# Wide cross-attention layers: SyncE's order of stores and fetches, three buffers for packed and turned probabilities, and VectorE's reciprocal ahead of its block transpose

## The reference

```python
def _L1_xattn_ref(hidden_states, encoder_hidden_states, Wq, Wk, Wv, Wo, bo):
    q = hidden_states @ Wq
    k = encoder_hidden_states @ Wk
    v = encoder_hidden_states @ Wv
    ...
    scores = jnp.einsum('bhsd,bhkd->bhsk', q, k) * Dh ** -0.5
    probs = jax.nn.softmax(scores, axis=-1)
    out = jnp.einsum('bhsk,bhkd->bhsd', probs, v)
    out = out.transpose(0, 2, 1, 3).reshape(B, S, H * Dh)
    return out @ Wo + bo
```

## Time and profile before

| | us |
|---|---|
| median of 3 runs | 1755.21 (1746.41 to 1760.99) |
| the profiled execution | 1738.73 |
| its span | 1736.9 |
| TensorE busy | 1450.2 (83%) |
| VectorE busy | 961.7 (55%) |
| ScalarE busy | 594.1 (34%) |
| GpSimd busy | 55.2 (3%) |

### The profile page before, as it was taken

How to read it: one execution, slowest core, us unless ns; L and a number is a source line. 1 busy time by engine, 2 the same in 40 slices (tenths; PEclk the granted TensorE clock), 3 DMA queues, 4 the chain that set the end, 5 groups by cost and what they waited for, 6 DMA issues and landing times.

```text
span 1736.9 us, 22426 instructions
## 1 busy us (share of the span) xinstructions
PE 1450.2 (83%) x9148; PEld 939.3 (54%) x9148; DVE 961.7 (55%) x1742; ACT 594.1 (34%) x850; POOL 55.2 (3%) x68
## 2 busy tenths in 40 slices
PE   5988798888988888798887888898887858877987
PEld 3555485355555455666473555455545528875444
DVE  5555603677767775233526667777762467733424
ACT  4512011455545544011014445545541105531302
POOL 0000000000000000000000000000000012220000
PEclk9998899989999998979788899999998859988987
DMA  5110153366667665600122566666764204552000
GB/s 198 76 49 1 49 200 140 109 182 169 174 166 187 173 174 160 197 1 1 73 97 64 154 184 179 170 172 173 190 182 149 106 25 154 199 203 75 1 1 12
DMA packets 102854, 215.86 MB, mean 124 GB/s; under 512 B 7776, under 2 KB 73312, under 8 KB 95200
## 3 DMA queue, kind: packets, MB, share of 16 engines
q1 hardware_dynamic: 101600, 206.04, 39.7%
q0 software_dynamic: 1152, 8.39, 1.3%
HBM read 146.77 MB, written 67.63 MB: 123 GB/s over the span
## 4 chain that ended last, share of the span: by engine, by line
PE 57%; DVE 19%; DMA 12%; issue 5%; SPq 4%; ACT 2%; POOL 1%; POOLq 0%; ACTq 0%; DVEq 0%
PE ps L237 26%; DMA ring<-blocks 11%; SPq L453 3%; DVE wk L941 3%; PE ps L1668 3%; DVE wk L944 3%; PE ps L1669 3%; PE ps L1670 3%; DVE wk L929 3%; PE ps L1553 2%; PE ps L1648 2%; PE ps L1696 2%; PE ps L1681 2%; PE ps L1612 2%; PE ps L1649 2%
## 5 line engine op out<-in xcount | busy, mean ns | idle before, releaser
L929 DVE TENSOR_REDUCE wk<-ps 128x1 f32<-128x1024 f32 x128 | 156.2, 1220 | 204.5 <-PE ps L1654 203.2
L599 ACT ACTIVATE wk<-wk 128x1024 f16<-128x1024 f32 x128 | 184.1, 1439 | 217.8 <-DVE wk L936 188.6
L590 ACT ACTIVATE wk<-ps,wk 128x1024 f32<-128x1024 f32 x128 | 142.1, 1110 | 169.2 <-DVE wk L929 168.2
L941 DVE SCALAR_TENSOR_TENSOR wk<-wk 128x1024 f16<-128x1024 f32 x128 | 181.3, 1416 | 10.4 <-ACT wk L599 10.1
L1668 PE MATMUL ps<-ring,ctx_keys 128*128 128x256 f16 x240 | 84.8, 353 | 107.7 <-DMA ring<-blocks 107.7
L944 DVE STREAM_TRANSPOSE wk<-wk 128x1024 f32<-128x1024 f32 x128 | 159.4, 1246 | 4.4
L237 PE MATMUL ps<-wk,ring 128*128 128x128 f32 (+3 forms) x896 | 133.7, 313 | 29.5 <-issue 11.6
L237 PEld LDWEIGHTS ps<-wk,ring 128*128 128x128 f32 x896 | 119.0, 211 | 43.3 <-issue 25.1
L237 PE MATMUL ps<-ring,wk 128*128 128x256 f32 (+2 forms) x456 | 112.4, 401 | 4.8 <-DVE wk L1130 1.7
L237 PE MATMUL ps<-wk 16*64 16x64 f32 (+8 forms) x1172 | 93.5, 249 | 15.6 <-ACT wk L708 8.1
L1553 PE MATMUL ps<-cst 128*128 128x512 f16 x362 | 100.9, 435 | 1.2 <-PE ps L237 0.3
(11 more groups left out here) (328 smaller groups left out, 2320.4 us busy)
## 6 DMA issues: line engine op xcount, KB each, us to landing
blocks<-wk SPq DMA_DIRECT2D x128, 512.0 KB, 3.1
ring<-units SPq DMA_DIRECT2D x34, 1024.0 KB, 6.0
xn_both<-blocks SPq DMA_DIRECT2D x128, 256.0 KB, 5.5
ring<-blocks SPq DMA_DIRECT2D x120, 256.0 KB, 5.3
ring<-experts SPq DMA_DIRECT2D x16, 1024.0 KB, 7.0
ring<-context SPq DMA_DIRECT2D x16, 384.0 KB, 3.8
wk<-context SPq DMA_DIRECT2D x16, 384.0 KB, 3.2
wk<-blocks SPq DMA_DIRECT2D x8, 256.0 KB, 5.8
```

What stands on the lines that cost most here:

```text
L590: ACTE.activation(blocks, bank(2 * (t % 2), 2, 4, 128), ACT.Exp, bias=WNM[:, t % 4:t % 4 + 1], accum_out=WRS[:, t % 4:t % 4 + 1]).then_inc ...
L599: ACTE.activation(WPH[:, t % 2, :], WXP[:, t % 2, :], ACT.Identity, scale=WRI[:, t % 4:t % 4 + 1]).then_inc(xa_PH, 1)
L929: DVE.tensor_reduce(WNM[:, t % 4:t % 4 + 1], bank(2 * (t % 2), 1024), X, ALU.max, negate=True).then_inc(xa_max, 1)
L941: DVE.scalar_tensor_tensor(WPL[:, t % 2, :], WXP[:, t % 2, :], WRI[:, t % 4:t % 4 + 1], WPH[:, t % 2, :], ALU.mult, ALU.subtract).then_inc ...
```

## The change

Six edits, the first four inside the wide layers:

1. The packed probabilities have three places, t % 3, at 6144, 7168 and 10252 of `wk`, which grows by 452 columns; `weights_high(t)` waits for the store of unit t-3.
2. The turned groups have three places in turn: the slot of Wo, `xn_both`, the slot of Wq; groups 30 and 31 take `xn_both` and Wq's slot. The fetch of group g waits for `attend_low(g-3)` (g-2 for the last two). Wo is loaded after unit 59's store and the fetch behind it, once `attend_low(27)` is done.
3. The fetch of group g stands behind the store of unit 2g + 1, one store earlier in SyncE's list.
4. VectorE does `recip(s)` before the block transpose of unit s-1, which has become a function of its own.
5. The constants are 316 columns narrower: `nhalf` has 4 columns where it had 64, and the two biases share one place of 256 columns. SyncE loads the second bias ahead of unit `L2x_k`, after the first has been added.
6. GpSimd waits for that load before it adds the bias.

```diff
+        def packed_weights(t):
+            return wv((6144, 7168, 10252)[t % 3], 1024)
+
+        def weight_halves(t):
+            v = packed_weights(t).bitcast(F16).rearrange("p (b h) -> p b h", h=2)
+            return v[:, :, 0], v[:, :, 1]
...
             if g == 0:
                 return wv(8192, 2, 1024)
-            if g % 2:
+            place = g % 3 if g < 30 else g - 29
+            if place == 1:
                 return xn_both[:, :].rearrange("p (j m) -> p j m", j=2)
-            return unit("L1x_q" if k == 0 else "L2x_q", 0, 2, 1024)
+            u = "L1x_" if k == 0 else "L2x_"
+            return unit(u + ("q" if place == 2 else "o"), 0, 2, 1024)
...
-                if g >= 2:
-                    sp.wait_ge(xa_Z, 2 * (32 * k + g - 2) + 2)
+                if g >= 4:
+                    sp.wait_ge(xa_Z, 2 * (32 * k + g - (3 if g < 30 else 2)) + 2)
...
-            def turn_weights(k):
-
+            def turn_weights(k, n):
+
+                sp.wait_ge(units_used, n - NSLOT + 1)
                 for t in range(64):
                     store_blocks(k, t)
-                    if t >= 2 and t % 2 == 0:
-                        fetch_turned(k, t // 2 - 1)
-                fetch_turned(k, 31)
+                    if t % 2 == 1:
+                        fetch_turned(k, t // 2)
+                    if t == 59:
+                        sp.wait_ge(xa_Z, 2 * (32 * k + 27) + 2)
+                        load(n)
...
-                load(n)
+                if UNITS[n] == "L2x_k":
+                    sp.wait_ge(xa_bo, NT)
+                    sp.dma_start(C("Lx_bo"), const_d[:, NCONST:]).then_inc(consts_loaded, 16)
                 if UNITS[n] in ("L1x_o", "L2x_o"):
-                    turn_weights(0 if UNITS[n] == "L1x_o" else 1)
+                    turn_weights(0 if UNITS[n] == "L1x_o" else 1, n)
+                else:
+                    load(n)
...
                     act.wait_ge(xa_recip, 64 * k + t + 1)
-                    if t >= 2:
-
-                        act.wait_ge(xa_stored[j], 16 * (32 * k + g))
-                    ACTE.activation(WPH[:, t % 2, :], WXP[:, t % 2, :], ACT.Identity,
+                    if t >= 3:
+
+                        act.wait_ge(xa_stored[(t - 3) % 2], 16 * (32 * k + (t - 3) // 2 + 1))
+                    ACTE.activation(weight_halves(t)[0], WXP[:, t % 2, :], ACT.Identity,
...
+
+                def block_transpose(t):
                     dve.wait_ge(xa_PL, 64 * k + t + 1)
-                    DVE.transpose(WPB[:, t % 2, :], WPB[:, t % 2, :]).then_inc(xa_block, 1)
+                    DVE.transpose(packed_weights(t), packed_weights(t)).then_inc(xa_block, 1)
...
                         weights_low(s - 1)
                     if s < 64:
                         recip(s)
+                    if s >= 1:
+                        block_transpose(s - 1)
```

27 lines of the change are left out of this document (14 added, 13 removed), and 1 row of the table _at.

## The result

| | before | after |
|---|---|---|
| runs measured together, median (us) | 1758.1 (1746.4, 1755.2, 1761.0, 3433.0) | 1614.3 (1596.1, 1598.8, 1629.8, 1632.1) |
| the profiled execution, its span | 1738.7, 1736.9 | 1596.1, 1594.3 |
| TensorE's granted clock, whole span | 0.898 | 0.937 |
| both wide layers | 884.6 | 765.1 |
| all the rest of the span | 852.3 | 829.2 |

A forecast was written before the change was run, and what follows sets the result against it. Fetches issued about 3.8 us late by their place in SyncE's list were taken to hold TensorE up. At 10.5 us a pair, 48.2 + 45.5 + 2 x 3.8 - 2 x 1.1 + 0.4 = 99.5 us saved: 1656, range 1612 to 1704.

The forecast's parts named there:

- The latency over two pairs: Wide layers, from `attend_high(g)` over odd store and next fetch to landing: 19.2 us for two pairs, 9.6 each, not binding.
- the closed cycle of transfers: Wide layers, one fetch and two stores, next fetch after the second store lands: 8.0 + 1.2 + 1.3 = 10.5 us a pair.
- P: Time of a pair of steps in the wide layers, from one group to the next; forecast 10.5 us.
- The place in SyncE's list: Fetch moved from behind store 2g+2 to behind store 2g+1: the part that pays; fetches were issued about 3.8 us late.
- The first group: Group 0 of each wide layer was to land at 331.5 instead of 335.28, 3.8 us earlier.
- T: Start of `attend_high(g)` in a wide layer; the fetch of g+2 was to land at T + 19.2.
- TensorE's floor: TensorE's own work in a pair of steps of the wide layers, keys and heads included: 9.9 us.
- The rival that TensorE becomes the bound: Wide layers: stores overlap the fetch well, pair time falls to 9.9, gain 135.5, time 1620 us; chance 0.22.
- 729.5 - 60 P: General formula for the whole gain in us, with P the time of a pair of steps.
- T30: Time from group 29 to group 30 in a wide layer; forecast 10.5 + 2.7 = 13.2 us, before 12.1.
- The price of 2.7 us for Wo: Wide layers: Wo, loaded behind fetch 29, adds 2.7 us to group 30's fetch; 1.1 us lost a layer.
- The third packed place: Third packed buffer in the wide layers: gains nothing alone, and is what the moved fetch needs.

The follow-up runs named there:

- e2: Changed kernel with the fetch put back behind store 2g+2, stores counted by three semaphores; median 1763.3 us, ratio 1.0167 to the kernel before.
- e4: Changed kernel with two packed and two turned places, Wo first, transpose before reciprocal, leaving only the fetch's new place and narrower constants; 1623.1 us, 0.921 of before.
- e7: Changed kernel with seven of eight low-half products for the context's second part left out of `attend_low`; 1599.1 us in one run.
- e9: Changed kernel with each fetch split into eight DMAs, the even unit's four leaving before the odd store has landed; median 1588.3 us.
- e1: Changed kernel with no edit, profiled a second time in another set of runs; median 1628.9 us.
- e8: Changed kernel with two of a fetch's four quarters left out from group 6 on; 1602.4 us in one run.
- e10: Changed kernel with the split fetch, two turned places and Wo loaded first; median 1578.2 us, 0.909 of the kernel before.
- e5: Changed kernel with two turned places instead of three and Wo loaded first; median 1610.5 us, 0.916 of the kernel before.
- e13: Changed kernel with filler matmuls ahead of four TensorE waits in block 1's feed-forward layer; median 1600.8 us.
- e14: Changed kernel with split fetch, two turned places, Wo first and four fillers in block 1's feed-forward layer; median 1559.8 us, 0.896 of the kernel before.
- e6: Changed kernel with the block transpose ahead of the reciprocal on VectorE again; median 1606.3 us, 0.922 of the kernel before.
- e3: Changed kernel with two packed places instead of three; median 1633.3 us.

## Why the prediction was right and wrong

**What failed, in short.** Two steps. The latency over two pairs, put at 9.6 us a pair, "alone would not bind"; it measures 9.95, and together with the times when TensorE is the later one it sets the pace, while the closed cycle of transfers, put at 8.0 + 1.2 + 1.3 = 10.5 and taken for the pace, binds nowhere. The measured P is 10.26, so this is worth 14 us. And the layers that the change does not touch were put at nothing, with no allowance for their own spread. This is what took the time below the range: with the 119.5 us of the wide layers alone it would be 1755.2 - 119.5 = 1636. Of the 38 us from there to 1598, 23 are the other layers in the profiled execution; the other 15 come from the side of before, whose profiled execution was itself 16.5 us quicker than its median.

**The place in SyncE's list pays: right.** e2 loses everything without it, e4 has 110.9 of 119.5 us with nothing else. The fetch leaves 0.1 us or less behind the odd store's landing, and in front of the even store, as said. The first group was to be read at 331.5 and is read at 331.48, but that is luck: store 1 left at 320.89 where it had been 319.95, and the way from there took 10.6 us (in both layers) where 11.6 was said, since the fetch took 7.9 and not 8.7. The 15.3 and 15.1 us of before have lost 4.7 and 4.5, not 3.8. The wait of 3.8 us that the change was to remove was that of group 10; in the mean over groups 3 to 28 the fetches of even groups left 3.1 us behind the odd store's landing and those of odd groups 0.5. The clock rose (0.92 to 0.99) and the DMA share went to 0.76, where 0.74 was said. The waits of `attend_high` were to be under 1 us and alike on odd and even groups; beside the first groups and groups 30 there are 24, of which 18 stand before even groups and 9 are over 1 us (up to 2.4).

**The cycle of the DMA engines: named as the pace, and it is not.** The step put it at 8.0 + 1.2 + 1.3 = 10.5. A fetch takes 7.3 us in the mean over groups 3 to 28, where it took 8.1 before (from its issue to the last quarter's landing). The rows before had it always right behind a store, 0.45 us behind in the median; e2, which puts it back there, has the slow quarters again. I had looked at the fetches' landings without asking what ran beside them, and in the new order nothing is under way when it leaves; the even store follows 1.9 us later. The even store lands 1.1 us behind the fetch (1.2 was said), the odd one 2.8 in the mean and 2.15 at least (2.5 was said). So the fetch was put 0.7 us too long and the stores 0.3 too short. But the fetch before does not hold the next one up: in the profile after the two fetches at 478.38 and 487.92 are 9.54 apart, and others 9.21. And the cycle is not closed by transfers: every odd store of the profile leaves 0.03 us behind its transpose, whatever the transfers do.

**The latency over two pairs: this step failed.** It was put at T + 19.2, or 9.6 a pair, and then set aside. The largest error in its terms is the odd store's, which was to land 2.6 us behind its issue. In the rows shown, `attend_high` starts at 486.01, the odd store leaves at 495.14 (T + 9.1; 8.8 was said), the fetch at 498.07 (2.9 behind it), and with 7.3 to land that is T + 19.4. In the mean over groups 3 to 28 of both layers the odd store takes 3.4 us, with the even store and the end of the fetch still there, and the loop comes to 2.7 + 2.15 + 4.2 + 3.4 + 7.4 = 19.9, or 9.95 a pair (7.4: a fetch of 7.3 and twice 0.05 us from a landing to what waits for it, where 7.8 was said; 4.2: from the end of the scores to the odd store, where 3.9 was said). That this loop goes through TensorE and VectorE can be read from the trace: in 51 of 52 groups the odd store leaves 8.94 to 9.2 us behind the start of `attend_high` two groups before. That is above TensorE's own 9.76, and it is what e7 to e9 show from three sides: with TensorE relieved P stays, with half the fetch or an earlier start it falls to 9.74 to 9.77. Between 9.95 and the measured 10.26 there are 0.3 us. In the mean a group has landed 0.53 us before its `attend_high` starts (0.46 in e1), because TensorE is still at work: half of that a pair. So now the one and now the other is late; 24 of the 52 groups are read within 0.1 us of their landing, and the rest wait for TensorE. That the uneven pairs of TensorE (10.74 to 8.74) are the cause of this was argued and not tried. e8 and e9 relieve the transfers too; what tells the loop from the cycle of transfers is the time of the odd store.

**TensorE's floor: 9.9 said, 9.76 measured** (e9, e10). The rival that TensorE becomes the bound gave 1620, and its time is nearer to the measured one than the forecast's; but in the changed kernel TensorE is the bound of some of the pairs only (e7, e8). It happens in e9.

**What a P of 10.26 gives.** By 729.5 - 60 P the gain would be 114 us. T30 was P + 2.7, or 13.2 at the forecast; by the measured P it would be 12.96 twice, and 11.2 and 10.4 were measured, 4.3 us less in all. With the 1.6 that the first groups gained beyond the sum this makes 120, and the wide layers gained 119.5. The price of 2.7 us for Wo is of the right size and no more: T30 is 10.4 to 13.5 in the two profiles of the changed kernel and 8.2 to 9.0 with Wo first (e5), so from 1.4 to 5.3; what was off is that a whole P was put in front of it.

**Outside the wide layers: nothing was forecast.** Measured were 23.1 us less in the profile after: 8.6 in the self-attention of block 1, 7.3 in its feed-forward layer, and 2.9, 3.3 and 1.6 in three others. It is no effect that comes with the change each time: e10 has 4.6 us more than before there, and e1, the changed kernel itself, 13.3. So of the 43 us by which the profiled execution lies under my 1639, 20 are the wide layers (14 from P over 58 pairs, 5 from T30) and 23 the layers behind. What decides in the feed-forward layer, 55.5 or 76.9 us, is made likely by e13 and e14. For the self-attention (115.4 us at 0.86 before, 106.8 at 0.94 after) nothing was tried. The lesson for the range is that it was built from P alone, while the unchanged layers differ by 36 us between two profiles of the same kernel (829.2 after, 865.6 in e1). By the four runs of e1, with a median of 1628.9, the forecast of 1656 would have been 27 off and inside its range; that the first profile was one of the three below 1600 us (of eight in all) was luck, as far as the runs tell.

**The other parts.** The third turned place at nothing: right (e5). The reciprocal's order at nothing: right (e6), though ScalarE's waits fell by 136 us. The third packed place "is what the first part needs": too strong; two places leave a wait of 174 us on ScalarE, and 17 to 20 us of it arrive (e3). The constants at 0.4 us: too small to be told apart.

**The page on DMA.** The Trainium skill, "DMA: Bandwidth & Descriptors", Specifications, gave 435 GB/s, by which the transfers of a pair would take 5 us (an estimate) and never be felt. The trace moves 209 GB/s in the stretch after and 218 in e10 with TensorE never waiting; a fetch of 1 MB takes 7.3 us. So the page's outcome, TensorE as the bound, came with e9 and not by its figure: a fetch of 7.3 us can be hidden when it may start early enough.

## What to carry to other kernels

Where a queue is worked off in order, look for the instruction whose data is ready and whose place in the list is behind one that isn't: moving one fetch by one store was worth 111 us of both wide layers here, and the extra buffers beside it next to nothing. Then follow the loop that is left, term by term, with each transfer at the time it takes among its new neighbours and not among its old ones; and if it binds by its length, let the part whose data is ready leave first. Costs of layers that the change doesn't touch belong to the range, by the difference between two executions of them.

## What the runs showed of the hardware

- A store of 512 KB lands 2.6 us behind its issue at the least, and 6.4 us (the one at 480.28) when a fetch of 1 MB was issued just before it; a fetch lands in 7.3 us with the queue empty and in 8.1 when a store was issued 0.45 us before it. Two transfers at once cost each other less than their sum: fetch and both stores, 7.3 + 2.6 + 2.6 = 12.5 us one after the other, fit into 9.54.
- Twice as many DMAs for the same bytes did no harm here. SyncE issues the second four of a split fetch while the first four move; from the first issue to the last landing such a fetch takes 7.6 us where it took 7.3, and the pair's time fell from 10.26 to 9.76.
- TensorE's clock can stay at 1.2 GHz long behind a short stall. In e10 a stall of 2.17 us is followed by 47.8 us at 0.50 of full, over 192 matmuls of 128x64 float32 with a stall of 0.90 us among them and one of 1.38 behind them; in the profile after, the same instructions with a stall of 2.02 us go on at 2.4 GHz. This makes 21 us in one layer, 1.4% of the kernel, at the same instructions. Matmuls that nothing reads, put into the layer's last four stalls, went with a clock of 0.95 in the profiles of both kernels that had them (56.9 and 57.1 us); put into the first of them alone, a fall came behind the next. Which of two executions falls is not known from these runs. The Trainium skill, "TensorE: Matmul & The Clock Gate", in the part on the HAM clock gate, says of the warm-up at a kernel's start that for modelling "the ramp penalty is <1% of a typical kernel span". The falls here come in the middle of a kernel, and what they cost in this layer alone is above 1% in five of the profiles.
